# Sharing part of an f16 split between VectorE and GpSimd in an attention kernel

## What is computed

```python
y = layernorm(x)                      # heads of 8 channels, q = k = y
scores = einsum('bhtk,bhsk->bhts', y, y) / sqrt(8)
o = einsum('bhts,bsc->bhtc', softmax(scores), y)    # values are all 128 channels
x = x + layernorm(o.transpose(...).reshape(b, t, 16 * 128) @ weight)
# then a gated feed-forward of width 128 on layernorm(x), layernorm, residual
```

## Time and profile before

| | |
|---|---|
| runs | 992.82, 991.94, 987.48 us; median 991.94 |
| profiled execution | 988.09 us, of which the span is 986.3 us |
| mean granted TensorE clock | 0.98 of full speed |
| instructions | 17700 |

### The profile page before, as it was taken

The page is one execution under the profiler, slowest core; times in us unless marked ns, Lnnn a source line. Parts: engine busy times, 40 slices in busy tenths (PEclk is TensorE's granted clock), DMA queues, the critical chain, the costliest instruction groups (busy, mean ns, idle before and its releaser), DMA issues.

```text
span 986.3 us, 17700 instructions
## 1 busy us (share of the span) xinstructions
PE 915.8 (93%) x5979; PEld 438.9 (44%) x5979; DVE 858.7 (87%) x1125; ACT 761.6 (77%) x1045; POOL 308.7 (31%) x490
## 2 busy tenths in 40 slices
PE   3789999999999999999999999999999999999992
PEld 2234444544444444444444444444444444444451
DVE  6579998889889998889898899979989898988976
ACT  5378778877888788878877879787788878777764
POOL 2012221442124521534117531265114441173210
PEclk9789999999999999999999999999999999999996
DMA  5699999989888988899897898988989897988830
GB/s 137 143 223 196 202 192 206 208 190 201 172 176 177 188 163 171 166 230 203 170 184 161 183 182 164 182 197 194 205 164 188 184 189 160 186 164 180 168 65 22
DMA packets 99466, 173.50 MB, mean 176 GB/s; under 512 B 21297, under 2 KB 62129, under 8 KB 99377
## 3 DMA queue, kind: packets, MB, share of 16 engines
q0 software_dynamic: 36720, 133.71, 70.3%
q1 hardware_dynamic: 62656, 38.67, 14.3%
HBM read 28.12 MB, written 10.49 MB: 39 GB/s over the span
## 4 chain that ended last, share of the span: by engine, by line
PE 58%; POOL 11%; ACT 9%; issue 9%; DVE 8%; DMA 5%; SPq 1%; DVEq 0%; POOLq 0%; ACTq 0%
PE ps_o L587 16%; PE ps_o L588 14%; PE ps_o L589 14%; POOL fnw L387 7%; PE ps_s L568 6%; ACT e_f L746 5%; DMA e_hi<-e_f 4%; DVE e_lo L1076 3%; PE ps_r L604 2%; PE ps_r L602 2%; PE ps_r L603 2%; POOL e_hi L422 2%; POOL nw L387 1%; ACT part L758 1%; ACT L746 1%
## 5 line engine op out<-in xcount | busy, mean ns | idle before, releaser
L1076 DVE TENSOR_TENSOR e_lo<-e_f,e_hi 128x2048 f16<-128x2048 f32 x256 | 584.9, 2285 | 60.9 <-DMA e_hi<-e_f 60.2
L746 ACT ACTIVATE e_f<-ps_s 128x2048 f32<-128x2048 f32 x256 | 481.7, 1882 | 143.3 <-PE ps_s L568 136.1
L587 PE MATMUL ps_o<-e_hi,y_hi 128*128 128x512 f16 x1024 | 394.3, 385 | 6.1 <-DVE o_neg L1082 6.0
L588 PE MATMUL ps_o<-e_lo,y_hi 128*128 128x512 f16 x1024 | 391.9, 383 | 0.0
L589 PE MATMUL ps_o<-e_hi,y_lo 128*128 128x512 f16 x1024 | 391.3, 382 | 0.0
L422 POOL DMA_DIRECT2D e_hi<-e_f x255 | 139.2, 546 | 615.4 <-ACT e_f L746 557.9
L758 ACT ACTIVATE part<-ps_r,rden 128x128 f32<-128x128 f32 x508 | 144.4, 374 | 33.3 <-DVE rden L1088 32.9
L587 PEld LDWEIGHTS ps_o<-e_hi,y_hi 128*128 128x128 f16 x1024 | 100.1, 98 | 157.3 <-issue 59.1
L589 PEld LDWEIGHTS ps_o<-e_hi,y_lo 128*128 128x128 f16 x1024 | 100.7, 98 | 123.3 <-issue 3.9
L588 PEld LDWEIGHTS ps_o<-e_lo,y_hi 128*128 128x128 f16 x1024 | 100.8, 98 | 93.3 <-issue 3.5
L568 PE MATMUL ps_s<-op_t,op_s 32*128 32x512 f16 x1024 | 103.0, 389 | 30.5 <-ACT e_f L746 25.4
(11 more groups left out here) (216 smaller groups left out, 456.5 us busy)
## 6 DMA issues: line engine op xcount, KB each, us to landing
e_hi<-e_f POOLq DMA_DIRECT2D x255, 512.0 KB, 4.9
op_t<-scr_t SPq DMA_DIRECT2D x504, 32.0 KB, 3.7
op_s<-scr_s SPq DMA_DIRECT2D x504, 16.0 KB, 3.2
scr_s<-yT SPq DMA_DIRECT2D x12, 256.0 KB, 4.5
scr_t<-yT SPq DMA_DIRECT2D x12, 256.0 KB, 5.6
out_dram<-res SPq DMA_DIRECT2D x7, 256.0 KB, 4.5
xs<-in_L_attn_x_dram SPq DMA_DIRECT2D x3, 512.0 KB, 6.9
scr_s<-eighth SPq DMA_DIRECT2D x4, 256.0 KB, 4.2
```

The lines of the kernel that those rows point to most:

```text
L587: nc.tensor.matmul(dst, y_hi[:, b % 2, s, :], e_hi[:, ring, g, :], start=(q == 0 and g == 0), stop=False)
L588: nc.tensor.matmul(dst, y_hi[:, b % 2, s, :], e_lo[:, ring, g, :], start=False, stop=False)
L746: nc.scalar.activation(e_f[:, k % EF_RING], ps_s[:], ACT.Exp, scale=1.0 / ROOT).then_inc(weighed, 1)
L1076: dve.tensor_tensor(flat(e_lo[:, ring]), flat(e_f[:, k % EF_RING]), flat(e_hi[:, ring]), ALU.subtract).then_inc(split, 1)
```

## The change

In nine of the 32 iterations of a row, for quads 8 to 251, DVE computes only the first two of the four blocks of e_lo, and POOL computes the other two. POOL does so in iteration k for quad k - 2, right behind the issue of the cast of quad k, and before its row and batch work of that iteration. It waits for the landing of the quad's cast and for the products that last read the ring's place. PE waits, ahead of a shared quad's products, for POOL's part as well, and ACT, before it overwrites e_f of a shared quad four back, too.

```diff
--- before.py
+++ after.py
@@ -23,6 +23,7 @@
 EH_RING = 6
 OP_RING = 4
 SPAN = 41
+SHARED = (3, 5, 7, 16, 17, 18, 19, 25, 31)
 O_BITS = 13
 W_BITS = 12
 
@@ -160,7 +161,7 @@
         op_in = [sem(f"op_in_{i}") for i in range(OP_RING)]
         cast_in = [sem(f"cast_in_{i}") for i in range(EH_RING)]
         rounded = sem("rounded")
-        scored, weighed, split = (sem(s) for s in ("scored", "weighed", "split"))
+        scored, weighed, split, pool_split = (sem(s) for s in ("scored", "weighed", "split", "pool_split"))
         product, taken, o_split, projected = (sem(s) for s in ("product", "taken", "o_split", "projected"))
         den_ok, scaled, added = (sem(s) for s in ("den_ok", "scaled", "added"))
         row_added = sem("row_added")
@@ -215,6 +216,18 @@
                     now = [QUADS - first + 2 * (k - QUADS) + i for i in range(2)]
                 found += [(r, o) for o in now if 0 <= o < (SPAN if r < LAST_ROW - 1 else SPAN - 5)]
             return found
+
+        def shared(k):
+
+            return LAG + 4 <= k < QUADS - 4 and (k + 2) % PER_ROW in SHARED
+
+        def shared_to(k):
+
+            return sum(shared(i) for i in range(k + 1))
+
+        def quad_cast(k):
+
+            return 16 * (k // EH_RING + (k % EH_RING > 0))
 
         def pair(u):
 
@@ -421,6 +434,13 @@
                 ge(pool, split, k - EH_RING + 1)
                 nc.gpsimd.dma_start(flat(e_hi[:, ring]), flat(e_f[:, k % EF_RING])).then_inc(cast_in[ring], 16)
 
+            def share_quad(k):
+                ring = k % EH_RING
+                pool.wait_ge(cast_in[ring], quad_cast(k))
+                ge(pool, product, k - EH_RING + 1)
+                nc.gpsimd.tensor_tensor(flat(e_lo[:, ring, 2:4]), flat(e_f[:, k % EF_RING, 2:4]), flat(e_hi[:, ring, 2:4]),
+                                        ALU.subtract).then_inc(pool_split, 1)
+
             def root_row(i, r, part_):
                 pool.wait_ge(f_mean[i], r + 1)
                 if i == 0 and r == 0:
@@ -453,6 +473,8 @@
             for k in range(LAST):
                 if 0 < k < QUADS:
                     cast(k)
+                if shared(k - 2):
+                    share_quad(k - 2)
                 for r, o in rows_at(k):
                     row_part(o, r)
                 b, o = next_batch(k)
@@ -573,6 +595,8 @@
                 j, q = k // 2, k % 2
                 b, ring = batch_of(j), k % EH_RING
                 pe.wait_ge(split, k + 1)
+                if shared(k):
+                    pe.wait_ge(pool_split, shared_to(k))
                 if q == 0:
                     ge(pe, o_split, j - 1)
                     if j == 0:
@@ -743,6 +767,8 @@
             def weigh(k):
                 act.wait_ge(scored, k + 1)
                 ge(act, split, k - EF_RING + 1)
+                if shared(k - EF_RING):
+                    act.wait_ge(pool_split, shared_to(k - EF_RING))
                 nc.scalar.activation(e_f[:, k % EF_RING], ps_s[:], ACT.Exp, scale=1.0 / ROOT).then_inc(weighed, 1)
 
             def take_o(j):
@@ -1071,9 +1097,10 @@
                 if k == 0:
                     dve.wait_ge(rounded, 1)
                 else:
-                    dve.wait_ge(cast_in[ring], 16 * (k // EH_RING + (ring > 0)))
+                    dve.wait_ge(cast_in[ring], quad_cast(k))
                 ge(dve, product, k - EH_RING + 1)
-                dve.tensor_tensor(flat(e_lo[:, ring]), flat(e_f[:, k % EF_RING]), flat(e_hi[:, ring]),
+                n = 2 if shared(k) else 4
+                dve.tensor_tensor(flat(e_lo[:, ring, 0:n]), flat(e_f[:, k % EF_RING, 0:n]), flat(e_hi[:, ring, 0:n]),
                                   ALU.subtract).then_inc(split, 1)
 
             def split_o(j):
```

## The result

| | before | changed |
|---|---|---|
| median | 990.33 us (4 runs) | 1037.05 us (4 runs, 1036.42 to 1042.01) |
| ratio | | 1.048, 95% interval 1.044 to 1.051 |
| profiled execution | 988.09 us, span 986.3 | 1037.45 us, span 1035.6 |

The change costs 47 us. The prediction had the sign, but said 1002 us, with a range of 980 to 1016.

What follows compares the result with a forecast made beforehand. PE and DVE were both taken as near full, with DVE a bound only in short places. Terms 6.6 + 2.4 + 1.5 + 1.5 = +12 us gave 1000.1 from the profiled execution, 1003.9 from the median; forecast 1002, range 980 to 1016.

Steps and rivals of the forecast that it cites:

- my main term: Iterations 16 to 19, rows with a batch root: POOL's late nw delays DVE's normalising, then o_neg; 3.3 us each, 6.6 us.
- My first rival: DVE's relief shortens PE's waits for o_neg: 6 to 10 us faster, about 980 profiled or 984 median; chance 0.27.
- DVE itself comes out about even in these iterations: Iterations 16 to 19: DVE saves 4.3 us, is shut out for 8.0, has some 3.3 of other work beside that.
- the replay's rule: When POOL's subtract is given during a DVE split, DVE's next operation in line goes first; read from y_lo at 354.00.
- Rows 2 and 4 (6.6 us): The two rows with a batch root, iterations 16 to 19: POOL late, nw waited for, 3.3 us each.
- Odd rows (2.4): Rows 1, 3 and 5, no batch root there: PE waits for o_neg, 0.8 us each, bounds nothing and 1.4.
- rows 6 and 7: With row 0, rows without a batch or an earlier row: more room, 0.5 us each, 1.5 us in all.
- Iteration 25 (1.5): In two rows DVE's cast of y_hi is shut out and o_neg behind it late: 0.75 us each, 1.5 us.
- Quiet iterations (0): Iterations 3, 5, 7 and 31, 28 of the 68 shares: PE is full and both halves have cover, so no cost.
- PE's busy time stays: Whole kernel: PE's busy time, 915.8 us before, was to be unchanged in the changed kernel's profile.
- The fourth (POOL first): POOL goes first whenever given first; o_neg 2.4 us too late in each of seven rows, 17 us, about 1007; chance 0.13.
- The third: Turns cost wherever DVE is dense: 40 shares of iterations 16 to 19 and 25 at 0.93 us, 37 us, about 1027; chance 0.05.

Runs made afterwards that it cites:

- The run with DVE first: Changed kernel with one more wait: POOL begins its half of a quad only after DVE's half of the same quad; 1017.27 us, ratio 1.030.
- the runs with 32 and 36 shares: Changed kernel sharing only iterations 16 to 19 (32 quads), 1031.55 us, or only 3, 5, 7, 25 and 31 (36 quads), 997.29 us; one run each.

## Why the prediction was wrong

**Right.** That subtract and two-input operation take turns and do not overlap; the price of a turn (2.1 us alone, 1.22 for the half, both as measured; POOL's 478 us of busy time where I had 480); that PE's full stretches hide it (28 shares for 2.7 us); that the shares of iterations 16 to 19 would come out as PE's wait for o_neg, though my main term had it at the o_neg of iteration 23 and it came at that of 19; and that the relief has little to win. My first rival gave it 6 to 10 us, and freed of its price it is 7.

**The step that failed** is "DVE itself comes out about even in these iterations". It rested on the replay's rule that "DVE's next operation, already in line, went first", taken from one place, where a split was running when y_lo was given. The changed kernel has the other case. DVE has just done o_neg and the reciprocal, nothing with two SBUF inputs runs on it, and POOL, with its cast issued, is there 0.4 us before DVE's half. From then on POOL is ahead. And no row of the kernel before could show what two subtracts in line do to a waiting operation, as y_lo has none behind it: 5.5 us for a half of 1.2. The time shut out I had about right: 8.0 us a row, and in the third row it was 8.6. What failed is what I set against it: 4.3 us of relief, of which 2.1 counted ahead of that o_neg, and 3.3 us of other work beside the turns, of which none was: it stands in the same queue behind the operation that is shut out. So DVE came out 6.5 us late, not even. PE's wait for o_neg grew by 4 to 5.7 us in each of seven rows where I had 3.3 us in two, 0.8 in three and 0.5 in the rest. The run with DVE first shows what the wrong rule was worth: 17 to 20 of the 47 us.

**The terms, one by one.** Rows 2 and 4 (6.6 us): the wait came from DVE, not from POOL's nw, and at iteration 19. Odd rows (2.4), rows 6 and 7: "more room" was no argument, as rows 6 and 7 have gaps of 4.5 us like the others. Iteration 25 (1.5): about 7 where iterations 16 to 19 aren't shared, as z, which I hadn't thought of as an operation that contends, is then shut out; little in the changed kernel, where it isn't. Quiet iterations (0): 2.7.

**Left out altogether:** the clock. I wrote "PE's busy time stays"; it rose by 12.0 us, a quarter of the loss, since each long gap is followed by matmuls at the lower level.

**The rivals.** The fourth (POOL first) named the right event, o_neg late at iteration 19 in every row, and priced it at 2.4 us a row; it was 4 to 5.7, with the clock on top. The third had nearly the size (1027), by a price per share, which the runs with 32 and 36 shares refute: 1.4 and 0.3 us. The Trainium skill (SBUF — State Buffer, "Who interferes with whom") says that whoever issues first gets the shared pair; in the changed kernel at 320.48 and 320.84 the trace agrees, while by the starts of the rows at 329.24 and 329.62 it doesn't. The range failed because it took rival 3 as a thing outside, on the ground that one-input work lies beside the turns; in the third row none did.

## What to carry to other kernels

Moving elementwise work from DVE to POOL doesn't add the two engines' speeds when the operations have two SBUF inputs: DVE's time, the shut-out included, went up by 43 us here, not down by 72. Before pricing such a move, measure what the relief is worth by leaving the work out (7 us here); then ask what stands behind the longest operation of the other engine in the in-order queue, and keep its turns short and apart. Here PE, held up for 4 us and more, also paid in clock each time.

## What I had not expected of the hardware

- A DVE operation with two SBUF inputs can stand through two POOL subtracts with 0.53 us between them (5.55 us for 1.22 us of work).
- By the starts of the rows alone one can't tell who goes first: a sum given 0.38 us before a POOL subtract stood behind it (329.24 and 329.62), a half given 0.42 us before another went ahead (888.09 and 888.51).
- POOL's memset, which reads nothing, doesn't touch DVE's subtract (1.21 us) and sum (0.69), but shuts out DVE's tensor_scalar on f32 in SBUF (3.05 us for 1.1).
- A gap of 5.67 us on PE is followed by 4.6 us at a granted clock of 0.57.
